# Linear attention: values by token from halves of 64 tokens, the denominator as a column of ones beside v, y transposed by DMA

## The chip, the cores and the metric

One core of one Trainium2 chip. The time is device microseconds of one execution. Before: 1068.77 us, the median of three runs (1067.99 to 1069.69).

## The reference, cut to what matters

```python
qkv = x @ W_attn + b_attn                      # x: (8, 1024, 512), after a layer norm
q, k, v = jnp.split(qkv, 3, axis=-1)           # 16 heads of 32
q = elu(to_heads(q)) + 1.0
k = elu(to_heads(k)) + 1.0
def step(carry, inp):                          # over the 1024 tokens
    kv = kv + kt[..., :, None] * vt[..., None, :]
    ksum = ksum + kt
    num = einsum('bhi,bhij->bhj', qt, kv)
    den = einsum('bhi,bhi->bh', qt, ksum)[..., None] + 1e-6
    return ((kv, ksum), num / den)
x = x + (y @ W_proj + b_proj)
x = x + ffn(layernorm(x))                      # clip, round to fp8, times fp8 weight, + bias
```

## The kernel before

The 8192 tokens are 64 tiles of 128; eight tiles are one sequence. Four tiles make a group (16 groups), for which q, k and v are computed in 12 blocks of 12 matmuls of 512 columns: the f32 operands are split into two f16 parts, and three of the four products are kept. Eight blocks give q and k with features on partitions (`phi`: ACT does exp and relu, VectorE joins them), four give v with tokens on partitions (`v_out`). The blocks of the next group are spread over the four tiles of this one, three a tile (A, B and C below; `ahead`).

A tile n does this. `scores`: per head k times q, 32 features, the result S with key tokens on partitions and 128 query tokens on columns, four PSUM banks, one per head h of a group g. The mask: VectorE takes head 0 with a product, ACT copies heads 1 to 3 and POOL masks them in place (L941). `values`: first state times q (from the second tile of a sequence on), then v times the masked scores, into Y, 128 columns of the same four banks; features on partitions. `update`: the tile's k and v give a 32 x 32 addition to each head's state, for which `k_tokens` has transposed k; in the last tile of a sequence both are left out. VectorE multiplies Y with the inverse denominators (L703) into y. ACT copies y's high part (yh), POOL makes the low one (yl), `proj` multiplies them with W_proj in 12 matmuls. VectorE adds x and takes statistics (L604 to L609), POOL norms (L909, L911) and adds a bias (L957), ACT makes fp8 and bf16 copies (`t2`), a DMA transposes, `ffn` multiplies, ACT copies, VectorE adds (L720), SyncE stores. `ln1` and `ln1_parts` do the layer norm of tile n + 8 and its two f16 parts (POOL norms, ACT copies the high part, VectorE the low one, L621), which a DMA transposes into xt, four tiles at once.

The denominator of a group before: VectorE scans k along the tokens (L647, L649), POOL multiplies the sums with q (L936), four matmuls with a matrix `pick` sum over a head's features (`den`), ACT copies, VectorE inverts (L656); the inverse is split into three bf16 parts (`den_rest`, `den_third`, `den_top`, `den_middle`), and four matmuls with `lend` spread them over partitions (`lend_out`), ACT copies them to rden.

The order of every engine is written out by hand; waits are on semaphores. On PE a tile's order is: scores(n), block A, block B, (in a group's first tile spreading), k_tokens(n + 1), block C, values(n), update(n), proj(n - 1), ffn(n - 2). scores(n + 1) waits for y(n). The PSUM has four banks R, taken in turn by every other product (`take`), and the four of S. On SyncE's queue: transposes of xt (four at a group's end), x2's transpose, the load of x for tile n + 10, the store of tile n - 2, each behind its wait. In the head the maxima of the three parts of W_attn are taken by VectorE (L732), scales are made (L741 to L751) and the weights are split; in tile 0 VectorE has W_proj's low part (L797) and four steps on the FFN weight (L803 to L816).

## Time and profile before

| | us |
|---|---|
| median of 3 runs | 1068.77 |
| profiled execution | 1068.26 |
| its span, first to last instruction | 1066.4 |
| TensorE (PE) busy | 995.8 (93%) |
| VectorE (DVE) busy | 772.3 (72%) |
| GpSimd (POOL) busy | 715.0 (67%) |
| ScalarE (ACT) busy | 570.8 (54%) |
| granted TensorE clock, mean | 0.985 |

The profile has the start and the duration of every instruction of one execution. PE is the matmuls, PEld the weight loads beside them; ends of matmuls are modelled, and they overlap, so start-to-start differences are used for their pace. A f32 matmul call leaves two records. In a timeline, each row is a start, a duration, engine, line, operation, output and inputs, and a count of merged records; brackets show how long the engine was idle before it and which instruction ended that.

### The profile page before, as it was taken

How to read it: one execution, taken by the hardware profiler on the slowest of the kernel's cores; microseconds unless marked ns; L12 is line 12 of the kernel's file. 1: busy time of each engine (PE TensorE's matmuls, PEld its weight loads, DVE VectorE, ACT ScalarE, POOL GpSimd, SP SyncE). 2: the span in 40 equal slices, each digit the busy share in tenths (PEclk: the TensorE clock that was granted, in tenths of full speed). 3: DMA queues.
4: the chain of work that ended last, by engine and by line, in shares of the span. 5: the costliest groups of instructions: out<-in, count | busy, mean ns of one | idle time of the engine just before them, and what ended most of it. 6: DMA issues, size and time to landing. Idle time of an engine off the chain costs nothing.

```text
span 1066.4 us, 27817 instructions
## 1 busy us (share of the span) xinstructions
PE 995.8 (93%) x11456; PEld 508.4 (48%) x11456; DVE 772.3 (72%) x1279; ACT 570.8 (54%) x937; POOL 715.0 (67%) x717
## 2 busy tenths in 40 slices
PE   5866999999999999999999999999999999999986
PEld 2323454455545545454544555455454554445542
DVE  7895777778777776877777687777767777775655
ACT  4444455564646555474655647465564746546442
POOL 4343969776785867678587767758667785864444
PEclk9988999999999999999999999999999999999989
DMA  8401131324123131313323231321313123121011
GB/s 263 102 1 41 46 71 41 76 52 80 46 61 70 42 75 51 80 41 66 61 51 76 51 72 44 71 60 51 76 51 67 49 65 66 41 66 31 22 41 51
DMA packets 121935, 65.78 MB, mean 62 GB/s; under 512 B 102480, under 2 KB 102480, under 8 KB 121808
## 3 DMA queue, kind: packets, MB, share of 16 engines
q1 hardware_dynamic: 121808, 63.99, 25.3%
q8 instruction: 91, 1.49, 0.6%
q14 instruction: 36, 0.29, 0.1%
HBM read 22.81 MB, written 16.78 MB: 37 GB/s over the span
## 4 chain that ended last, share of the span: by engine, by line
PE 49%; POOL 30%; DVE 11%; ACT 5%; issue 3%; DMA 1%; SPq 0%; POOLq 0%; DVEq 0%; ACTq 0%
PE R L220 40%; POOL sm L941 9%; POOL st L909 6%; PE S L220 5%; POOL xs L957 5%; POOL xs L926 4%; POOL xn L911 3%; POOL x L911 3%; DVE xs L710 3%; DVE st L604 3%; PE S L308 2%; ACT rel L445 1%; ACT qkv L442 1%; PE R L224 1%; ACT xnhl L430 1%
## 5 line engine op out<-in xcount | busy, mean ns | idle before, releaser
L220 PE MATMUL R<-xt,wh 128*128 128x512 f16 x960 | 289.2, 383 | 14.0 <-ACT rel L445 14.0
L627 DVE SCALAR_TENSOR_TENSOR qkv<-qkv,rel 128x512 f32<-128x512 f32 x128 | 117.3, 917 | 142.2 <-ACT rel L445 142.1
L941 POOL TENSOR_SCALAR_AFFINE_SELECT sm<-sm 128x512 f32<-128x512 f32 x184 | 181.5, 1014 | 5.4 <-ACT sm L430 5.4
L220 PE MATMUL R<-xt,wl 128*128 128x512 f16 x480 | 183.2, 382 | 0.0
L909 POOL TENSOR_TENSOR st<-st,half 128x1 f32<-128x1 f32 x128 | 93.5, 731 | 133.3 <-DVE st L609 127.4
L936 POOL TENSOR_TENSOR cum<-cum,qkv 128x512 f32<-128x512 f32 x64 | 88.0, 1375 | 102.0 <-DVE cum L647 56.1
L220 PE MATMUL R<-wh,xt 128*128 128x512 f16 x480 | 150.3, 379 | 0.0
L220 PEld LDWEIGHTS R<-xt,wh 128*128 128x128 f16 x960 | 89.4, 98 | 120.7 <-ACT rel L445 17.5
L442 ACT ACTIVATE qkv<-R,bqk,wm 128x512 f32<-128x512 f32 x128 | 99.5, 777 | 69.6 <-PE R L220 68.7
L948 POOL TENSOR_TENSOR yl<-y,yh 128x512 f16<-128x512 f32 x64 | 74.9, 1170 | 80.0 <-ACT yh L430 79.1
L430 ACT ACTIVATE yh<-y 128x512 f16<-128x512 f32 x64 | 40.3, 630 | 136.8 <-DVE y L703 136.8
L430 ACT ACTIVATE sm<-S 128x512 f32<-128x512 f32 x184 | 96.9, 598 | 29.4 <-PE S L308 29.1
L621 DVE TENSOR_TENSOR xnhl<-xn,xnhl 128x512 f16<-128x512 f32 x60 | 74.8, 1247 | 33.3 <-ACT xnhl L430 33.2
L926 POOL TENSOR_TENSOR xs<-xs,bp 128x512 f32<-128x512 f32 x64 | 95.5, 1492 | 4.7
L445 ACT ACTIVATE rel<-R,bqk,wm 128x512 f32<-128x512 f32 x128 | 98.5, 769 | 0.0
L710 DVE SCALAR_TENSOR_TENSOR xs<-R,wm,xs 128x512 f32<-128x512 f32 x64 | 48.0, 750 | 66.6 <-PE R L220 66.6
L604 DVE BATCH_NORM_STATS2 st<-xs 128x6 f32<-128x512 f32 x128 | 88.4, 690 | 6.5 <-DMA xs<-in_L_attn_x 4.2
L220 PE MATMUL R<-wl,xt 128*128 128x512 f16 x240 | 91.0, 379 | 0.0
L430 ACT ACTIVATE o<-R 128x512 f16<-128x512 f32 x64 | 38.2, 596 | 97.8 <-PE R L220 97.8
L220 PE MATMUL S<-sm,qkv 128*32 128x128 f32 x2048 | 77.5, 277 | 12.2 <-POOL sm L941 12.1
L308 PE MATMUL S<-qkv 32*128 32x128 f32 x2048 | 77.4, 289 | 9.4 <-DVE y L703 9.4
L957 POOL TENSOR_TENSOR xs<-xs,bf 128x512 f32<-128x512 f32 x64 | 81.7, 1276 | 5.3
(107 smaller groups left out, 1705.8 us busy)
## 6 DMA issues: line engine op xcount, KB each, us to landing
xs<-in_L_attn_x SPq DMA_DIRECT2D x64, 256.0 KB, 3.1
out<-xs SPq DMA_DIRECT2D x64, 256.0 KB, 2.0
qkv<-in_L_attn_W_attn SPq DMA_DIRECT2D x3, 1024.0 KB, 7.9
xs<-in_L_attn_W_proj SPq DMA_DIRECT2D x4, 256.0 KB
rden<-in_L_ffn_weight SPq DMA_DIRECT2D x1, 1024.0 KB, 14.7
x2t<-x2b SPq DMA_TRANSPOSE x62, 2.4
xt<-xnhl SPq DMA_TRANSPOSE x60, 3.2
bv<-in_L_attn_b_attn SPq DMA_DIRECT2D x1, 256.0 KB, 8.1
```

Source lines behind the costliest of these rows:

```text
L220: return e.matmul(out, a, b, start=start, stop=stop, skip_group_check=True)
L308: mm = e.matmul(S[:, h, g * P:(g + 1) * P], src[rows, 4 + g, cols], src[rows, g, cols], start=True, stop=True)
L430: return e.activation(out, in_, ACT.Copy, **more)
L442: e.activation(dst[:, i, :], bank["qkv", j, i][:, :], ACT.Exp, scale=UN[i // 4], bias=bqk[:, i:i + 1])
L445: e.activation(rel[:, u % 2, :], bank["qkv", j, i][:, :], ACT.Relu, scale=UN[i // 4], bias=bqk[:, i:i + 1]).then_inc(s_relu, 1)
L604: e.bn_stats(row[:, 0:6], src).then_inc(s_bn, 1)
L627: e.scalar_tensor_tensor(qkv[j % 2][:, i, :], qkv[j % 2][:, i, :], 1.0, rel[:, (u - 1) % 2, :], ALU.min, ALU.add).then_inc(s_phi, 1)
L909: e.tensor_tensor(row[:, 10:11], row[:, 9:10], half[:, :], ALU.pow).then_inc(s_rs, 1)
L926: e.tensor_tensor(x, x, bp[:, :], ALU.add).then_inc(s_xb, 1)
L936: e.tensor_tensor(c, c, qkv[j % 2][:, g, :], ALU.mult).then_inc(s_qc, 1)
L941: e.affine_select(out=four(sm[:, h, :]), in_=four(sm[:, h, :]), compare_op=ALU.is_ge, fill=0.0, base=0, pattern=[[0, 4], [1, P]], channel_ ...
L957: e.tensor_tensor(x, x, bf[:, :], ALU.add).then_inc(s_x1b, 1)
```

## The change

- Tokens lie on the partitions of the result. A tile is two halves of 64 tokens. `scores` gives for each half its own 64 x 64 block, in two column strips. A half's effect on the next one goes through the state: `update` gives an addition for each half, VectorE makes `mid` (the state after the first half) and `state`. `from_state` multiplies q of each half with the state before that half.
- v has a column of ones beside each head (`W` = 33 columns), so the state has the sums of k as a 33rd column, and Y has the denominator as a 33rd column. VectorE adds epsilon, inverts 16 numbers a partition and multiplies. The scans, `den`, the inverse's parts and `lend_out` are gone; k_tokens and update are made for all tiles.
- y has tokens on partitions and its two parts are transposed by a DMA (`t_y` on SyncE). For the last four tiles PE transposes y and ACT and VectorE make the parts.
- ACT copies two of four heads' scores in one instruction and POOL masks them with a product; VectorE masks the other two. In the last four tiles VectorE masks all.
- update moves to the tile before, `proj` stands behind `values` in the last group too. xt has two buffers, and is transposed one tile at a time, behind y's transpose on SyncE's queue.
- Head: ACT measures the size of the first two parts of W_attn and of W_proj (a sum of absolute values), VectorE keeps the maximum for v, now ahead of `scale(1)`; POOL clips the FFN weight and makes the low parts of x for tiles 4 to 7. `ffn_low` stands ahead of tile 0, `ffn_high` in it ahead of values, `ffn_round` behind update(1), `ffn_sum` in tile 1. ACT's `ffn_half` and `proj_weight` stand ahead of tile 0.

```diff
 NT = B * T // P
 NB = NT // 4
...
         UN_V, UN_P = wm[:, 33:34], wm[:, 34:35]
-        raw = qkv[1][:, :, :].rearrange("p a n -> p (a n)").rearrange("p (k n) -> p k n", k=4)
         raw_p = xs[:, NX - 4:NX, :]
-        xt0 = sm[:, :, :].rearrange("p a n -> p (a n)").bitcast(F16).rearrange("p (k n) -> p k n", k=8)
-        w_f = rden[1][:, :, :]
...
-                for h in heads:
-                    out = take(("lent", 4 * j + h), s_rden, 4 * j + h + 1)
-                    pe.wait_ge(s_lend, 4)
-                    pe.wait_ge(s_third, j + 1)
-                    matmul(out[:, :], lend[:, h, :], inverse(j)[2], True, True).then_inc(s_lent, 1)
-
...
+            def update(n):
...
+                passes = n % PER < PER - 1
+                out = [take(("delta", n, 0), s_mid, n + 1)]
+                if passes:
+                    out.append(take(("delta", n, 1), s_state, state_count(n)))
...
+                for g in range(4):
+                    for a in range(len(out)):
+                        rows = tokens(n, a)[1]
+                        for h in range(4):
+                            at = 4 * g + h
+                            mm = matmul(out[a][32 * h:32 * h + 32, g * W:(g + 1) * W],
+                                        ktok[rows, n % 2, 32 * at:32 * at + 32], v[rows, c, at, :], True, True)
+                mm.then_inc(s_delta, 1)
...
-                    for h in range(4):
-                        rows = slice(32 * h, 32 * h + 32)
-                        mm = e.matmul(S[:, h, g * P:(g + 1) * P], src[rows, 4 + g, cols], src[rows, g, cols],
-                                      start=True, stop=True)
-                        if g == 3:
-                            mm.then_inc(s_score, 1)
...
-                for g in range(4):
-                    for h in range(4):
-                        at = (4 * g + h) * 32
-                        mm = matmul(out[32 * h:32 * h + 32, 32 * g:32 * g + 32], ktok[:, n % 2, at:at + 32],
-                                    src[:, 8 + c, at:at + 32], True, True)
...
+                    for a in range(2):
+                        cols, out = tokens(n, a)
+                        for h in range(4):
+                            rows = slice(32 * h, 32 * h + 32)
+                            matmul(S[out, h, g * HALF:(g + 1) * HALF], src[rows, 4 + g, cols], src[rows, g, cols], True, True)
...
+                for a in range(1 if first else 0, 2):
+                    cols, out = tokens(n, a)
+                    held = mid if a else state[:, n % 2, :]
                     for g in range(4):
                         for h in range(4):
                             rows = slice(32 * h, 32 * h + 32)
-                            matmul(Y[32 * g:32 * g + 32, h, :], state[rows, n % 2, 32 * g:32 * g + 32],
-                                   src[rows, g, cols], True, False)
+                            mm = matmul(Y[out, h, g * W:(g + 1) * W], src[rows, g, cols], held[rows, g * W:(g + 1) * W],
+                                        g == 0, False)
+                            if a == 1 and g == 3:
+                                mm.then_inc(s_score, 1)
+
+            def values(n):
...
                 for h in range(4):
-                    if h >= dve_heads(n):
-                        pe.wait_ge(s_sel, masked_act(n, h))
                     for g in range(4):
-                        col = (4 * g + h) * 32
-                        mm = matmul(Y[32 * g:32 * g + 32, h, :], src[:, 8 + c, col:col + 32],
-                                    sm[:, h, g * P:(g + 1) * P], first, True)
+                        for a in range(2):
+                            rows = tokens(n, a)[1]
+                            mm = matmul(Y[rows, h, g * W:(g + 1) * W], sm[rows, h, g, :], v[rows, c, 4 * g + h, :],
+                                        first and a == 0 and g == 0, True)
                 mm.then_inc(s_av, 1)
+
+            def t_y(n):
+                out = take(("ty", n), s_ytl, n - NT + 5)
+                pe.wait_ge(s_y, n + 1)
+                transposes(out, [y[:, h * P:(h + 1) * P] for h in range(4)]).then_inc(s_ty, 1)
 
...
-                    mm = matmul(out[:, :], yl[:, n % 2, g * P:(g + 1) * P], wph[:, g, :], False, g == 3)
...
+                    pe.wait_ge(s_yt[n % 2], 16 * (n // 2 + 1))
+                mms = [(a + h, b, h) for a, b in ((0, wph), (0, wpl), (4, wph)) for h in range(4)]
+                for i, (k, b, h) in enumerate(mms):
+                    mm = matmul(out[:, :], yt[:, n % 2, k, :], b[:, h, :], i == 0, i == 11)
...
                 proj_qkv(0, i)
-                if i in (0, 2):
-                    most(1 if i == 0 else 2)
-            k_tokens(0)
-            den(0)
-            most(3)
+                if i in (0, 2, 8):
+                    most((0, 2, 8).index(i) + 1)
+                if i == 9:
+                    k_tokens(0)
+            update(0)
             for n in range(NT + 2):
...
                 if n < NT:
                     scores(n)
+                    from_state(n)
                     ahead(j + 1, 3 * c)
-                    if j + 1 == NB:
-                        proj(n - 1)
...
-                    if c == 0:
-                        lend_out(j, (0, 1))
...
+                if n <= NT and tail(n - 1):
+                    t_y(n - 1)
...
-                    if c == 0:
-                        lend_out(j, (2, 3))
                     values(n)
-                    update(n)
-                if 1 <= n < NT and j + 1 < NB:
+                    if n + 1 < NT:
+                        update(n + 1)
+                if 1 <= n <= NT:
                     proj(n - 1)
                 if n >= 2:
+                    t2(n - 2)
                     ffn(n - 2)
...
             def scores(n):
-                for h in range(dve_heads(n), 4):
-                    act.wait_ge(s_score, 4 * n + h + 1)
+                if not tail(n):
+                    act.wait_ge(s_score, 4 * n + 4)
                     if n:
                         act.wait_ge(s_av, n)
-                    else:
-                        act.wait_ge(s_qkv, 12)
-                    copy(sm[:, h, :], S[:, h, :]).then_inc(s_scopy, 1)
+                    copy(sm[:, 2:4, :, :], scored(2)).then_inc(s_scopy, 1)
...
             def scores(n):
-                for h in range(dve_heads(n)):
...
+                for i, h in enumerate((0, 2) if tail(n) else (0,)):
...
-                    e.tensor_tensor(four(sm[:, h, :]), four(S[:, h, :]), over(causal[:, :]),
-                                    ALU.mult).then_inc(s_smd, 1)
+                    e.tensor_tensor(sm[:, h:h + 2, :, :], scored(h), causal_over(2), ALU.mult).then_inc(s_smd, 1)
 
...
+                    e.tensor_copy(mid[:, :], fresh).then_inc(s_mid, 1)
+                else:
                     dve.wait_ge(s_state, state_count(n - 1))
-                new, old, fresh = state[:, (n + 1) % 2, :], state[:, n % 2, :], bank["delta", n][:, 0:P]
-                if n % PER == 0:
-                    e.tensor_copy(new, fresh).then_inc(s_state, 1)
-                else:
-                    e.tensor_tensor(new, fresh, old, ALU.add).then_inc(s_state, 1)
+                    e.tensor_tensor(mid[:, :], fresh, old, ALU.add).then_inc(s_mid, 1)
+                if n % PER < PER - 1:
+                    dve.wait_ge(s_mid, n + 1)
+                    e.tensor_tensor(new, bank["delta", n, 1][:, 0:4 * W], mid[:, :], ALU.add).then_inc(s_state, 1)
...
+                e.tensor_scalar(inv, out[:, :, :, 32:33], DEN_EPS, None, ALU.add).then_inc(s_den, 1)
+                dve.wait_ge(s_den, n + 1)
+                e.reciprocal(den[:, :], den[:, :]).then_inc(s_dinv, 1)
...
-                e.tensor_tensor(four(y[:, :]), Y, rden[j % 2][:, :, c * P:(c + 1) * P],
-                                ALU.mult).then_inc(s_y, 1)
+                e.tensor_tensor(y[:, :].rearrange("p (h g i) -> p h g i", h=4, g=4), out[:, :, :, 0:32],
+                                inv.broadcast_to([P, 4, 4, 32]), ALU.mult).then_inc(s_y, 1)
+
...
-            for g in range(4):
-                denominators(0, g)
-                v_out(0, g)
-            parts_less()
-            proj_peak()
-            invert(0)
-            den_rest(0)
+            ffn_low()
+            v_out(0, 0)
+            v_out(0, 1)
             proj_scale()
-            den_third(0)
+            v_out(0, 2)
+            v_out(0, 3)
+            update(0)
...
-                    if j + 1 == NB:
-                        proj(n - 1)
+                    if n == 1:
+                        ffn_sum()
...
-                    if n == 0:
-                        ffn_low()
...
-                    if c == 3 and j + 1 < NB:
-                        invert(j + 1)
...
-                    update(n)
-                    if c == 3 and j + 1 < NB:
-                        den_rest(j + 1)
-                if 1 <= n < NT and j + 1 < NB:
+                    if n + 1 < NT:
+                        update(n + 1)
+                    if n == 0:
+                        ffn_round()
+                if 1 <= n <= NT:
                     proj(n - 1)
                 if n >= 2:
...
-                for h in range(dve_heads(n), 4):
-                    pool.wait_ge(s_scopy, masked_act(n, h))
-                    e.affine_select(out=four(sm[:, h, :]), in_=four(sm[:, h, :]), compare_op=ALU.is_ge, fill=0.0,
-                                    base=0, pattern=[[0, 4], [1, P]], channel_multiplier=-1).then_inc(s_sel, 1)
+                if not tail(n):
+                    pool.wait_ge(s_scopy, n + 1)
+                    e.tensor_tensor(sm[:, 2:4, :, :], sm[:, 2:4, :, :], causal_over(2), ALU.mult).then_inc(s_sel, 1)
...
+            for k in range(4):
+                e.tensor_scalar(w_f[:, k, :], w_f[:, k, :], 448.0, -448.0, ALU.min, ALU.max).then_inc(s_wfc, 1)
...
+                    if n + 8 < NT:
                         add_bp(n + 8)
-                    scores(n)
...
-                    after(j + 1, 3 * c + 2)
                     values(n)
...
+            def t_y(n):
...
+                    sp.wait_ge(s_yl, n + 1)
+                    if n >= 2:
+                        sp.wait_ge(s_proj, n - 1)
+                    e.dma_start(yt[:, n % 2, :, :], yhl[:, n % 2, :, :].rearrange("p a n -> p (a n)"),
+                                transpose=True).then_inc(s_yt[n % 2], 16)
...
             for n in range(NT + 2):
-                j, c = divmod(n, 4)
-                last = c == 3 and j + 2 < NB
-                if last:
-                    t1(4 * j + 8)
-                    t1(4 * j + 9)
+                if 1 <= n <= NT:
+                    t_y(n - 1)
...
+                if n + 8 < NT:
+                    t1(n + 8)
                 if n >= 2:
                     t2(n - 2)
...
-                if n == 0:
-                    sp.wait_ge(s_wfd, 5)
```

## Rows read from the trace of the kernel before

**Rows 1.** The page: the span, and busy time, share and instructions of two engines
```profile
span 1066.4 us, 27817 instructions
...
PE 995.8 (93%) x11456; PEld 508.4 (48%) x11456; DVE 772.3 (72%) x1279; ACT 570.8 (54%) x937; POOL 715.0 (67%) x717
```
**Rows 2.** Windows: three tiles; busy us and instructions per engine, clock, DMA
```profile
577.05:593.04 15.99, 15.32 (x157) 7.95 (x156) 10.91 (x19) 11.87 (x20) 10.26 (x11) 1.00 0.18 54
...
623.71:639.56 15.85, 15.85 (x193) 7.95 (x192) 11.98 (x19) 6.36 (x11) 9.43 (x11) 1.00 0.53 94
982.97:997.68 14.71, 14.71 (x185) 7.88 (x184) 9.65 (x14) 7.33 (x12) 8.86 (x9) 1.00 0.10 29
```
**Rows 3.** Waits from 184 to 960 us: total us, times, longest
```profile
PE S L220 <- POOL sm L941: 10.3, 23, 0.6
...
PE R L220 <- ACT rel L445: 8.1, 12, 0.7
```
**Rows 4.** Timelines of the head, PE first, then DVE: start us, us, instruction
```profile
31.00 0.55 PE L220 MATMUL R<-ident,wm 128*128 128x128 f32 x2 [4.37 <-DVE wm L732]
...
59.01 1.06 PE L220 MATMUL R<-cum,pick 128*32 128x512 f32 x8 [2.12 <-POOL cum L936]
61.22 0.46 PE L220 MATMUL R<-ident,wm 128*128 128x128 f32 x2 [1.15 <-DVE wm L732]
61.61 1.17 PE L308 MATMUL S<-qkv 32*128 32x128 f32 x32
...
90.68 2.09 PE L308 MATMUL S<-qkv 32*128 32x128 f32 x32 [9.40 <-DVE y L703]
...
28.57 2.28 DVE L732 TENSOR_REDUCE wm<-qkv 128x1 f32<-128x2048 f32 x1
...
76.67 3.35 DVE L797 SCALAR_TENSOR_TENSOR wpl<-xs,wm,wph 128x2048 f16<-128x2048 f32 x1
...
83.83 2.61 DVE L811 SCALAR_TENSOR_TENSOR x<-x 128x2048 fp8e4<-128x2048 fp8e4 x1 [0.89 <-ACT x L430]
```
**Rows 5.** Timeline of PE at the tail: scores of tile 60
```profile
1013.54 1.17 PE L308 MATMUL S<-qkv 32*128 32x128 f32 x32
```
**Rows 6.** Timelines of PE in windows 992.39:992.49, 982.97:983.86, 993.72:993.94 (records started)
```profile
992.39 0.39 PE L220 MATMUL S<-qkv,state 32*32 32x128 f32 x16
...
982.97 1.15 PE L308 MATMUL S<-qkv 32*128 32x128 f32 x29
...
993.72 0.43 PE L220 MATMUL R<-qkv,ktok 128*32 128x32 f32 x28
```
**Rows 7.** Groups of weight loads by line: busy us, mean ns, idle before
```profile
L308 PEld LDWEIGHTS S<-qkv 32*128 32x128 f32 x2048 | 64.9, 191 | 36.3 <-issue 26.3 <-DVE y L703 9.9
...
L220 PEld LDWEIGHTS R<-qkv,ktok 128*32 128x32 f32 x1792 | 26.5, 111 | 0.0
```
**Rows 8.** Timeline of PE in a late tile
```profile
992.39 0.50 PE L220 MATMUL S<-qkv,state 32*32 32x128 f32 x32
992.82 1.10 PE L220 MATMUL S<-sm,qkv 128*32 128x128 f32 x32
993.72 0.48 PE L220 MATMUL R<-qkv,ktok 128*32 128x32 f32 x32
994.13 1.04 PE L220 MATMUL R<-wph,yh 128*128 128x512 f16 x4
```
**Rows 9.** Timeline of POOL in a tile of the steady state
```profile
594.31 0.93 POOL L909 TENSOR_TENSOR st<-st,half 128x1 f32<-128x1 f32 x1 [0.61 <-DVE st L609]
...
598.93 1.59 POOL L926 TENSOR_TENSOR xs<-xs,bp 128x512 f32<-128x512 f32 x1
600.48 3.64 POOL L941 TENSOR_SCALAR_AFFINE_SELECT sm<-sm 128x512 f32<-128x512 f32 x3
```
**Rows 10.** DMA issues by kind: KB each, median us from issue to landing
```profile
x2t<-x2b SPq DMA_TRANSPOSE x62, 2.4
```

More of the change, by code:

```diff
@@ L19 @@
 P = 128
+HALF = P // 2
+W = 33
 NT = B * T // P
@@ L158, in build @@
         s_xt = [sem(f"xt{t}") for t in range(4)]
+        s_yt = [sem(f"yt{i}") for i in range(2)]
         s_x2t = [sem(f"x2t{i}") for i in range(2)]
-        s_t1, s_qkv, s_den, s_lent, s_score = sem("t1"), sem("qkv"), sem("den"), sem("lent"), sem("score")
-        s_ktr, s_delta, s_av, s_proj = sem("ktr"), sem("delta"), sem("av"), sem("proj")
-        s_ffn, s_t2, s_most = sem("ffn"), sem("t2"), sem("most")
-        s_xth, s_wh, s_relu, s_whi = sem("xth"), sem("wh"), sem("relu"), sem("whi")
@@ L525, in values @@
             def values(n):
-                act.wait_ge(s_y, n + 1)
-                if n >= 2:
-                    act.wait_ge(s_proj, n - 1)
-                copy(yh[:, n % 2, :], y[:, :]).then_inc(s_yh, 1)
+                if not tail(n):
+                    act.wait_ge(s_y, n + 1)
+                    if n >= 2:
+                        act.wait_ge(s_yt[n % 2], 16 * (n // 2))
+                    copy(yhl[:, n % 2, 0, :], y[:, :]).then_inc(s_yh, 1)
+            def t_y(n):
+                act.wait_ge(s_ty, n - NT + 5)
+                act.wait_ge(s_proj, n - 1)
+                copy(yt[:, n % 2, 0:4, :], four(bank["ty", n][:, :])).then_inc(s_yth, 1)
             def ffn(n):
@@ L537, in ahead, with t1 @@
             def ahead(j, s):
-                if j < NB:
-                    if s < 8:
-                        phi(j, ORDER[s])
-                    if s == 10:
-                        den(j)
-            for m in range(4):
-                act.wait_ge(s_t1, m + 1)
-                copy(xt0[:, 0:4, m * P:(m + 1) * P], four(bank["t1", m][:, :])).then_inc(s_xth, 1)
+                if j < NB and s < 8:
+                    phi(j, ORDER[s])
+            def t1(m):
+                act.wait_ge(s_t1, m + 1)
+                copy(xt[0][:, 0:4, m * P:(m + 1) * P], four(bank["t1", m][:, :])).then_inc(s_xth, 1)
+            t1(0)
+            t1(1)
+            t1(2)
+            attn_size(0)
+            t1(3)
             attn_weight(0)
             attn_weight(1)
+            attn_size(1)
             phi(0, 0)
@@ L967, in _ @@
             e.memset(half[:, :], -0.5).then_inc(s_half, 1)
+            for i in range(2):
+                e.memset(v1[i][:, :, :, 32:33], 1.0).then_inc(s_one, 1)
             for m in range(4):
```

456 lines of the change are left out of this document (174 added, 282 removed).

## The prediction

> **What bounds the kernel now.** I read the page first [rows 1]: TensorE (PE) is busy for 93% of the span, VectorE (DVE) for 72%, the others for less. Ends of matmuls are modelled, so the 93% alone proves little. The pace of the tiles says more. [rows 2] cut one group of four tiles where the scores of a tile begin: 15.99 us for its first tile, 15.85 for its last, and 639.56 - 577.05 = 62.51 for the four. The last row there is a tile late in the run, where GpSimd (POOL) has no more layer norms of later tiles to make: 14.71 us, with PE busy in all of it. So 14.71 us is what PE needs for a tile. [rows 3] name the waits that make up the rest: between 184 and 960 us PE stood idle 10.3 us behind POOL's masking of scores and 8.1 us behind ACT's relu. In a group, 4 x 14.71 = 58.85 are tiles, 15.85 - 14.71 = 1.14 the sums of the denominator, four spreading matmuls of 512 columns (512 / 2.4 = 213 ns and 3 between) another 0.87: 60.9. The other 1.6 are waits. PE is the bound, and all waits together are under 3%.
>
> The head is another matter: tile 0's scores begin at 61.61 us and tile 1's at 90.68 [rows 4], 29.07 us for one tile. The tail, from tile 60's scores to the end, is 1066.4 - 1013.54 = 52.9 us [rows 1, 5].
>
> **The change part by part.** The sum stands against the profiled execution's own 1068.26 us, of which 1066.4 are span and 1.9 lie around it; the median of the runs is 0.5 higher.
>
> *How small f32 matmuls run.* One call is two records. [rows 6] show stages cut short: of the state products (32 x 32 of the array) 16 records start within 0.10 us, 6.6 ns apart. Of the scores (four row strips; 128 columns moving, 128 of weights) 29 start in 0.89 us: eight rounds of four, 0.111 each. Of the state's update (four column strips; 32 columns of each) 28 start in 0.22 us: eight rounds of 0.032. So a round costs the longer of moving (two cycles of 2.4 GHz a column: 107 ns for 128, 27 ns for 32) and weights, plus 4 to 5 ns, and each array tile runs by itself. [rows 7]: a weight load takes 191 ns for 128 columns of f32 and 111 for 32, about 0.83 ns a column, so 64 columns have 53 ns. Behind a stage whose shape is left lie 0.11 to 0.2 us more.
>
> *Scores and state products.* Each is 32 calls now, 64 records, 64 columns of weights, 64 or 33 moving, on 4 x 2 array tiles. A round of eight is 0.057, each stage 0.46, one change of shape behind both: 1.05 us. Before they took 1.11 (the 0.89 of [rows 6] and 0.22 behind it) and 0.43 [rows 8]. **-0.49 us a tile.** The bound from above is the dearest row of a short record, the update with what lies behind it, 0.41 / 32 = 12.8 ns: 128 x 12.8 = 1.64, +0.10.
>
> *Values.* 32 calls with 64 rows and 64 columns of weights, 33 moving. Only the two array tiles of the diagonal are used, so it is 32 rounds of 0.057 = 1.83, plus 0.12 behind, as the update has another shape now: 1.95 against 0.90 [rows 8]. **+1.05.** Bounds: if weights didn't count, the update's round, 32 x 0.032 + 0.12 = 1.14 (+0.24); if the two tiles ran in turn, 64 x 0.057 + 0.12 = 3.77 (+2.87). I take 0.057, since in the scores' round weights and moving are equally long and neither adds to the other.
>
> *Update.* 32 calls on eight array tiles, 64 records at 6.6 ns and what lies behind: 0.57 against 0.41 [rows 8]. **+0.16.** Together +0.72: **14.71 + 0.72 = 15.43 us a tile.** In every eighth tile half the state product and in another half the update is missing, 14 x 0.22 = -3 us over the run.
>
> *Denominator and spreading, gone.* On PE 1.14 + 0.87 us a group; 15.43 is already without them. The scans, reciprocals, products and copies of DVE, POOL and ACT lie beside PE and bring nothing but the waits of [rows 3]. DVE gets two small operations and one more state addition a tile (some 0.2 us each); POOL masks by one product instead of 3.64 us of three selects [rows 9].
>
> *What is late next.* Count from the start of a tile's scores. PE: scores and state 1.05, blocks A and B 6.2, key transposes 6.7, C 9.3, values 11.25, update 11.8, proj 14.4, ffn 15.4. POOL's mask waits in its queue behind ln2 of the last tile, whose statistics DVE has at 1.3, and behind ln1: some 4.3 us (from 594.31 to the addition at 598.93, less a wait between, [rows 9]), and the product takes 1.6 like that addition: done at 7.2, needed at 9.3. DVE: phi C to 12.2, denominators and y to 13.4, states to 14.0; needed at 15.4. SyncE's queue now has y's transpose, then xt's, which waits for DVE's low parts (7.4), then x2's. y's own starts behind the store of the last tile but two (which waits for DVE's addition, about 2 us into the next tile) and lands at 6.7, needed at 11.8. x2's is issued when ACT has its copy, at 9.9, 1.2 us of issue and 2.4 to landing [rows 10]: 13.5, needed at 14.5. So every margin is 1 us or more. Where one goes, the tile costs what a wait costs now, 0.6 us (15.34 against 14.71). I take 0.1 a tile, 6 us; bounds 0 and 0.6.
>
> *Head.* PE waits 4.37 us up to 31.00 for the third weight's scale, because DVE takes its maximum (28.57) behind two phis; matmuls start at half pace behind that stall for some 3.5 us (clock 1.2 instead of 2.4 GHz). The maximum now comes ahead of the second scale: -4.4 and -1.5. A wait of 2.12 us for POOL's sums, den's 1 us and another wait for a scale lie between 59.01 - 2.12 and 61.61 [rows 4]; they go, while phi(7), the FFN weight's first part and v on one DVE queue hold block 10 for 1.1, and the update of tile 0 waits for the last block. Scores(0) then begin at 52.9: **-8.7.** In tile 0 DVE's queue sets y(0): 3.35 us for proj's weight, 2.61 and more for the FFN weight [rows 4]. Afterwards: phi A 6.1, low parts 7.4, phi B 8.9, proj's weight 12.3, phi C 13.0, the 2.6 to 15.6, y and states to 16.8. **16.8 - 29.07 = -12.3**, with PE still idle for 4.3 of it. Tile 1: no ffn (-0.95), half clock at its start (+1.5).
>
> *Tail.* Tiles 60 to 62 have no blocks; PE's own work is 8.3 us each and the chain of proj, statistics, ln2, two copies and a transpose sets about 9.5; with the masks on DVE alone and y transposed by PE the last tile has one more copy in its chain and less masking. I leave the tail at its 52.9 us [rows 1, 5]. **0, give or take 4.**
>
> *Sum.* Tile 1 begins at 52.9 + 16.8 = 69.7. 59 tiles of 15.43 are 910.4; +0.5 (tile 1), -3, +6 (waits): tile 60 at 983.6. With 52.9 and 1.9: **1038 us.**
>
> **The rivals.** (a) *Issue is the bound; slower.* No stage of now has more than 32 records at 6.6 ns in a row; scores and state products have 128. If a record costs 12.8 ns in a long row, then scores, state and update are 192 x 12.8 = 2.46, with values 4.41 against 2.85 now, 16.27 a tile: +50, **1088**. The sign turns where these four stages pass 4.1 us. Against it speak the 28 records in 0.22 us right behind 64 others [rows 6]; for it, that no row shows a longer stretch. The Trainium skill, page "TensorE: Matmul & The Clock Gate", section "Wait — 56ns, not 53.3ns?", says that starts are never closer than about 25 ns, however few the columns. The rows here show 13 ns for a call of two records. By the page, an estimate: 96 calls x 25 ns = 2.4 us, the same 1088.
>
> (b) *The two tiles of the diagonal exclude each other; slower.* Both row strips write bank h together, while now each row strip has its own bank. Values take 3.77: 1.83 x 59 = +108, **1146**. Against: writes last 27 ns of a round that weights hold to 57, so that writes in turn would still fit. The Trainium skill has a rule for it, page "TensorEngine Tiling", section "Gotcha 1: PSUM Pressure": different row tiles cannot access the same PSUM bank at the same time. No row here shows such a case.
>
> (c) *Weights of 64 columns don't count.* Values 1.14: -0.81 x 59, **990**. Against: [rows 7].
>
> (d) *A new wait in most tiles,* x2's transpose behind xt's, or y behind phi C: 0.6 for 0.1, +30 and something for the tail: **1073**. For it: margins of 1 us are thin.
>
> (e) *The steady pace isn't moved* (15.63 as now) and only the head is gained: 1068.3 - 21 = 1047, within the forecast's range.
>
> **How the numbers follow.** Forecast with (e) 0.60, its own range 1018 to 1062; (a) 0.16, (b) 0.08, (c) 0.07, (d) 0.09. The range leaves (b) and (c) out and takes (a) with its spread: 1012 to 1100. A measurement of this kernel tells 0.2% (2 us) from no change. Faster: 0.57 of the forecast's and (c), 0.64; same 0.04; slower 0.32.
>
> **What would show it.** Tile 0's scores at 53 us, tile 1's at 70. In a late tile, start to start: scores and state 1.05, values 1.95, update 0.57, the tile 15.4 to 15.6, no idle PE behind POOL's mask. (a) would show as scores and state over 1.6, (b) as values of 3.8, (d) as PE idle by over 0.5 us ahead of ffn or scores in most tiles. A pace over 15.9 us would make the sign wrong.

## The result and the profile after

The changed kernel took 1076.62 us, the median of 4 runs (1074.19 to 1077.97), the kernel before 1069.19 on the same chip: ratio 1.0069, 95% interval 1.0048 to 1.0089. Slower by 0.7%, where the forecast was 1038. The profiled execution had 1077.97, of which 1076.2 are span.

The page of the changed kernel, its first lines, with queue 8, which brings instructions, and the chain that ended last:

```profile
span 1076.2 us, 43457 instructions
...
PE 1048.8 (97%) x19504; PEld 616.9 (57%) x19504; DVE 648.9 (60%) x1319; ACT 458.3 (43%) x715; POOL 534.8 (50%) x524
...
q8 instruction: 153, 2.51, 1.0%
...
PE 93%; DVE 2%; POOL 1%; ACT 1%; issue 1%; DMA 1%; POOLq 0%
```

VectorE, ScalarE and POOL have less to do than in [rows 1], as the change says; PE has more: 19504 records for 11456, and 53 us of busy time more. The waits of [rows 3] are gone; between 184 and 960 us PE waits for nobody. But the pace did not fall. Windows of three whole tiles (columns as in [rows 2]):

```profile
584.16:600.33 16.17, 16.17 (x314) 9.57 (x313) 10.19 (x20) 8.30 (x13) 8.29 (x8) 1.00 0.30 72
...
972.52:988.69 16.17, 16.17 (x313) 9.57 (x312) 6.67 (x15) 7.71 (x12) 5.34 (x5) 1.00 0.16 43
988.69:1004.86 16.17, 16.17 (x313) 9.57 (x313) 6.81 (x15) 6.35 (x10) 5.33 (x5) 1.00 0.17 44
```

16.17 us with PE busy throughout, mid-run and late, for 14.71 unhindered and some 15.6 with waits before [rows 2]. Timelines of PE show the head, the tail and one tile:

```profile
54.92 0.81 PE L212 MATMUL S<-qk 32*64 32x64 f32 x53
70.18 0.41 PE L212 MATMUL S<-qk 32*64 32x64 f32 x8 [2.89 <-DVE y L649]
1021.03 0.31 PE L212 MATMUL S<-qk 32*64 32x64 f32 x8
```
```profile
966.29 2.06 PE L212 MATMUL S<-v,sm 64*64 64x33 f32 x64
968.27 0.76 PE L212 MATMUL R<-v,ktok 64*32 64x33 f32 x64
968.97 1.04 PE L212 MATMUL R<-wph,yt 128*128 128x512 f16 x4
...
972.52 0.86 PE L212 MATMUL S<-qk 32*64 32x64 f32 x60
973.16 0.21 PE L212 MATMUL S<-state,qk 32*64 32x33 f32 x1
...
974.15 0.39 PE L212 MATMUL R<-xt,wh 128*128 128x512 f16 x1
```

Start to start: values 968.27 - 966.29 = 1.98, update 0.70, scores and state 974.15 - 972.52 = 1.63. The same stages cut short, in windows 972.52:972.75 and 968.27:968.47, have the records that started by then:

```profile
972.52 0.44 PE L212 MATMUL S<-qk 32*64 32x64 f32 x25
...
968.27 0.35 PE L212 MATMUL R<-v,ktok 64*32 64x33 f32 x32
```

25 records of the scores in 0.23 us are 9 ns each, 32 of the update in 0.20 us 6 ns each.

The whole difference of the two profiled executions is then: head 70.18 - 90.68 = -20.5 [rows 4]; 59 tiles 1021.03 - 70.18 = 950.9 for 922.9 before [rows 4, 5], +28.0; tail 55.2 for 52.9, +2.3. Together +9.8, against 1076.2 - 1066.4 = 9.8 between the spans.

### The profile page after: what moved, and what is told of

Its sections match the earlier page's. It is cut to its first block, busy times and chain, and to the rows that moved or that the text cites. A ratio compares the mean times of both kernels' runs of the same rounds, so it can differ in the third digit from the quotient of the medians.

```text
span 1076.2 us, 43457 instructions
## 1 busy us (share of the span) xinstructions
PE 1048.8 (97%) x19504; PEld 616.9 (57%) x19504; DVE 648.9 (60%) x1319; ACT 458.3 (43%) x715; POOL 534.8 (50%) x524
## 4 chain that ended last, share of the span: by engine, by line
PE 93%; DVE 2%; POOL 1%; ACT 1%; issue 1%; DMA 1%; POOLq 0%
PE R L212 70%; PE S L212 21%; PE R L216 3%; POOL st L838 1%; DVE st L578 0%; POOL xn L840 0%; DMA x2t<-x2b 0%; DVE xs L661 0%; DVE sm L618 0%; POOL xnhl L853 0%; DMA xs<-in_L_attn_x 0%; DVE wl L716 0%; DVE raw L755 0%; ACT qk L426 0%; ACT wh L417 0%
## 5 line engine op out<-in xcount | busy, mean ns | idle before, releaser
L212 PE MATMUL R<-xt,wh 128*128 128x512 f16 x1024 | 307.1, 382 | 2.4 <-ACT wh L417 2.4
L601 DVE SCALAR_TENSOR_TENSOR qk<-qk,rel 128x512 f32<-128x512 f32 x128 | 131.1, 1025 | 170.1 <-ACT rel L429 170.0
L872 POOL TENSOR_TENSOR yhl<-y,yhl 128x512 f16<-128x512 f32 x60 | 70.1, 1168 | 322.0 <-ACT yhl L417 322.0
L426 ACT ACTIVATE qk<-R,bqk,wm 128x512 f32<-128x512 f32 x128 | 99.5, 777 | 121.4 <-PE R L212 121.3
L212 PEld LDWEIGHTS S<-v,sm 64*64 64x64 f32 x4096 | 124.5, 135 | 28.6 <-issue 25.4
L212 PE MATMUL R<-wph,yt 128*128 128x512 f16 x512 | 132.9, 382 | 2.0 <-DVE yt L654 2.0
L212 PE MATMUL S<-v,sm 64*64 64x33 f32 x4096 | 131.6, 221 | 2.3 <-DVE sm L618 2.3
L417 ACT ACTIVATE yhl<-y 128x512 f16<-128x512 f32 x60 | 37.8, 631 | 165.5 <-DVE y L649 165.5
L595 DVE TENSOR_TENSOR xnhl<-xn,xnhl 128x512 f16<-128x512 f32 x56 | 86.3, 1540 | 19.5 <-ACT xnhl L417 19.5
L212 PEld LDWEIGHTS R<-xt,wl 128*128 128x128 f16 x512 | 50.4, 98 | 61.4 <-issue 1.7
L212 PEld LDWEIGHTS R<-wh,xt 128*128 128x128 f16 x512 | 50.3, 98 | 56.4 <-issue 1.6
```

Source lines behind the costliest of these rows:

```text
L212: return e.matmul(out, a, b, start=start, stop=stop, skip_group_check=True)
L417: return e.activation(out, in_, ACT.Copy, **more)
L426: e.activation(dst[:, i, :], bank["qkv", j, i][:, :], ACT.Exp, scale=UN[i // 4], bias=bqk[:, i:i + 1])
L595: e.tensor_tensor(xnhl[:, m % 4, 1, :], xn[:, m % 2, :], xnhl[:, m % 4, 0, :], ALU.subtract).then_inc(s_xlo, 1)
L601: e.scalar_tensor_tensor(qk[j % 2][:, i, :], qk[j % 2][:, i, :], 1.0, rel[:, (u - 1) % 2, :], ALU.min, ALU.add).then_inc(s_phi, 1)
L872: e.tensor_tensor(yhl[:, n % 2, 1, :], y[:, :], yhl[:, n % 2, 0, :], ALU.subtract).then_inc(s_yl, 1)
```

## Experiments

All times beside "before" are from the same chip as the run they stand with. e2, e4, e7 and e8 are single runs. A "train" is a row of short products with nothing wide between them; a "stage" is one of a tile's steps on PE (scores and state, values, update, projection).

**e1 and e2: is it the order of the loops or the number of records?** In the state products the halves are the outer loop, so that only four array tiles follow each other, not the eight that the forecast counted. e1 puts them inside:

```diff
-for a in range(1 if first else 0, 2):
-    ...
-    for g in range(4):
-        for h in range(4): ...
+for g in range(4):
+    for a in range(1 if first else 0, 2):
+        ...
+        for h in range(4): ...
```

> The state products loop over g outside and the halves inside, so that eight array tiles follow each other instead of four; nothing else. Theory of tiles and queue: a record costs the round (57 ns for 64 columns of weights) over the number of array tiles that follow each other, and behind the first 32 records of a run not under 8.3 ns. The changed kernel's state products used four tiles (14.3 ns a record). Now 32 x 7.2 + 96 x 8.3 + 130 ns = 1.16 us for scores and state together against 1.63, in 56 of 64 tiles: -26 us, 1050. Rival, issue alone at 12 to 13 ns a record: nothing moves, 1077.

Measured 1067.78 (10 runs), before 1067.80: ratio 1.0003, 0.9991 to 1.0015. In the trace:

```profile
709.73 0.85 PE L212 MATMUL S<-qk 32*64 32x64 f32 x60
...
711.20 0.39 PE L212 MATMUL R<-xt,wh 128*128 128x512 f16 x1
```

1.47 for the 128 records. The order is worth 0.16 us a tile and 7 to 9 us in all (7 by the ratios to before, 9 by the medians, which are from different chips); 1.47 is still 0.42 over the forecast's 1.05, with eight array tiles in turn. It lies between the two values expected, 1.16 and 1.63, and bears neither theory out. e2 does the reverse in `scores`:

```diff
-for g in range(4):
-    ...
-    for a in range(2): ...
+for a in range(2):
+    for g in range(4): ...
```

> The scores loop over the halves outside, so that only four array tiles follow each other; nothing else. Tiles and queue: 64 records at 57 / 4 = 14.3 ns, 0.91 us against 0.70 up to the state's first record, +0.22 x 64 = +14 us, 1091. Issue alone: no change, 1077.

1082.66 in one run; the stage takes 1.73 for 1.63. The expectations were 0.22 us more and none; measured is 0.10. So four array tiles in turn cost 0.1 to 0.16 us a stage. The other 0.42 us is not the loops' order; it goes with the stage of 128 records, as rival (a) had it, but neither run shows why.

**e8: does a shorter train run faster?** The update's 64 records in two trains of 32, the second behind the projection.

```diff
-update(n + 1)
+update(n + 1, (0, 1))
 ...
 proj(n - 1)
+update(n + 1, (2, 3))
```

> The changed kernel with the update's 64 records issued as 32 ahead of the projection and 32 behind it. Theory of the queue (about 32 records start at 7 ns each, and only what follows them is paced by issue): each half's starts lie within 0.23 us, and the two halves take about 0.25 to 0.39 each with their last product, against 0.69 in one; the time is 1074 to 1080. Rival (the array's tiles pace the update, 9 to 11 ns a record whatever is queued): each half's starts spread over 0.29 to 0.35 us.

1087.34 in one run. Timeline of PE:

```profile
715.98 0.36 PE L212 MATMUL R<-v,ktok 64*32 64x33 f32 x32
...
718.96 0.36 PE L212 MATMUL R<-v,ktok 64*32 64x33 f32 x32
```

The next stage begins 0.29 us behind each start: 0.58 for what takes 0.69 in one. That is the update of the forecast (0.57). As expected, 32 records start within 0.2 us; in the one train of the changed kernel the first 32 start within 0.16 us and the last at 0.57 (medians of its tiles). The time, expected at 1074 to 1080, rose, by 9.4 us between the profiled executions. The projection now has 2.69 us from its start to the next stage's, not 2.60, so that most tiles take 16.16 for 16.17; PE waits six times, 4.7 us in all, for "issue" in `scores` and state; the tail is 2.4 us longer (57.6 for 55.2); and the tile of each sequence in which the update has only 32 records takes 16.1 for 15.87. The waits for issue belong to the next question but one.

**e4: do the two array tiles of the diagonal exclude each other?** The values' products, all of the first half, then all of the second, so that only one array tile is at work.

```diff
-for h in range(4):
-    for g in range(4):
-        for a in range(2): ...
+for a in range(2):
+    for h in range(4):
+        for g in range(4): ...
```

> Values does all calls of the first half, then all of the second: one array tile at a time, same calls. If the two diagonal tiles run beside each other in the changed kernel though they write the same bank: 64 x 57 ns + 0.12 = 3.77 us against 1.98, +1.79 x 64 = +115 us, 1192. If they take turns already (the rule on banks): no change, 1077.

1229.43 in one run:

```profile
706.61 3.71 PE L212 MATMUL S<-v,sm 64*64 64x33 f32 x64
710.25 0.83 PE L212 MATMUL R<-v,ktok 64*32 64x33 f32 x64
711.01 1.89 PE L212 MATMUL R<-wph,yt 128*128 128x512 f16 x4
...
726.04 3.71 PE L212 MATMUL S<-v,sm 64*64 64x33 f32 x64
729.68 0.76 PE L212 MATMUL R<-v,ktok 64*32 64x33 f32 x64
730.37 1.04 PE L212 MATMUL R<-wph,yt 128*128 128x512 f16 x4
```

3.64 in turn, 1.98 side by side, though both write the same bank. Rival (b) is out. The Trainium skill, page "TensorEngine Tiling", section "Gotcha 1: PSUM Pressure", forbids row tiles to share a bank at one time; in this kernel the two overlap and lose no time by it. The run is 37 us over the expectation, and 24 tiles of 59 account for that: they take some 19.5 us for 17.8. Behind the long narrow stage, in which PE used one array tile, the granted clock falls there to the lower level, 1.2 GHz. Windows (PE busy, clock, DMA): the first begins with the slow projection above, the second with the fast one.

```profile
711.01:714.20 3.19, 3.19 (x13) 0.51 0.03 5
730.37:732.97 2.60, 2.60 (x19) 1.00 0.02 6
```

**e3: do the weights' columns set the values?** Each values product in two of 32 columns, 128 records instead of 64, on four array tiles; the loops are those of the changed kernel:

```diff
-mm = matmul(Y[rows, h, g * W:(g + 1) * W], sm[rows, h, g, :], v[rows, c, 4 * g + h, :], ...)
+for b in range(2):
+    at = a * HALF + b * 32
+    mm = matmul(Y[at:at + 32, h, g * W:(g + 1) * W], sm[rows, h, g, b * 32:b * 32 + 32], v[rows, c, 4 * g + h, :], ...)
```

> Each call of values is split into two with 32 columns of weights, on two column strips: 64 calls, four array tiles, the shape of the update behind it. Tiles and queue: a round of four is 33 ns (weights 27), 8.2 ns a record, about the queue's 8.3, so 128 records take 1.07 us, no drain behind, the update 0.66: 1.73 against 2.67, -0.94 x 63 = -59 us, 1018. Issue alone at 12.6 ns: 1.61 + 0.8, -17 us, 1060. If weights are loaded one column strip after the other, nothing is won: 1077 or more.

1119.91 (4 runs), ratio 1.0489 (1.0466 to 1.0513). Timelines of two tiles, then the waits of the whole run (us in total, times, longest):

```profile
705.85 1.41 PE L212 MATMUL S<-v,sm 64*32 64x33 f32 x128
707.11 0.75 PE L212 MATMUL R<-v,ktok 64*32 64x33 f32 x64
...
720.97 1.40 PE L212 MATMUL S<-v,sm 64*32 64x33 f32 x128
722.22 0.55 PE L212 MATMUL R<-v,ktok 64*32 64x33 f32 x40
724.96 0.33 PE L212 MATMUL R<-v,ktok 64*32 64x33 f32 x24 [2.19 <-issue]
```
```profile
PE R L212 <- issue: 49.1, 28, 2.6
...
PE S L212 <- issue: 5.8, 8, 1.3
```

The narrower weights work: values in 1.26 for 1.98, and a whole tile without a wait takes 15.47 for 16.17 (the first of a sequence, which lacks half of the state products, 15.25 for 15.85). The records of such a train start at an even pace, the first 32 in 0.26 us and all 128 in 1.10 (medians of e10, which has the same train), 8.6 ns each; so a train of 128 need not take the 11.5 ns a record of scores and state in e1. The time expected was 1018, or 1060 if issue alone set the pace; it is 1120, because in other tiles PE stops in the middle of a train. No semaphore is waited for; the row says "issue".

**Where the waits stand.** I numbered TensorE's instructions (records, weight loads, waits of their own) in the order in which they started. In e3, e6, e8, e9, e10, e11 and e14 there are 84 waits for "issue" of over 0.5 us between 100 and 1060 us, and every one stands ahead of a number that leaves 193 on division by 256; I call these places borders. Each ended 1.1 to 1.6 us after one of queue 8's packets of 16384 bytes had landed. In e3, for one, a border lies in the values at 721.31; a packet starts at 722.11 and lands at 723.50, and PE goes on from the next border at 724.96. Windows between three waits of e3, from the first record behind one to the next wait, show it without numbering:

```profile
724.96:742.92 17.96, 15.78 (x382) 9.11 (x383) 10.07 (x20) 8.29 (x14) 8.05 (x9) 1.00 0.35 69
742.93:762.53 19.60, 17.48 (x383) 9.43 (x382) 10.45 (x20) 6.94 (x11) 8.81 (x9) 0.91 0.30 61
```

765 records and loads in either, and three waits of PE's own: 768 = 3 x 256. The Trainium skill, page "Runtime: NRT & Kernel Launch", section "Instruction fetch mechanics", says that instructions come in blocks of 16 KiB, 256 of them; the trace agrees. It also says that the fetch is hidden because issue is slower than the fetch; here it isn't. A train of 128 records has 256 instructions with its weight loads and passes in 1.26 us. Borders at which PE waited lie 2.3 to 7.9 us behind the last one, the middle one 3.6, wait included; without the wait itself 81 of the 84 lie under 3.5 us behind it. In the kernel before no two borders between 100 and 1000 us are nearer than 5.7 us by the same count. Nearness alone isn't the whole rule: the changed kernel has 13 borders under 3.5 us behind the last, the nearest 1.8, and waits at none.

**e6, e9, e10, e11: spread the trains.** All have e1's loop order. e6 is e3's values with the projection between values and update; e9 has only two of the four banks in 32 columns; e10 and e11 also have the projection there and move the tile's third block of wide products (C) behind the update, on ACT and VectorE too, e10 with all four banks, e11 with two. The order of a tile's end in e6 and in e10, e11:

```diff
 # e6
 values(n)
-update(n + 1)
 proj(n - 1)
+update(n + 1)
 ...
 # e10, e11
-ahead(j + 1, 3 * c + 2)
 values(n)
-update(n + 1)
 proj(n - 1)
+update(n + 1)
+ahead(j + 1, 3 * c + 2)
```

> The changed kernel with the halves inside the loop over heads' groups in the products with the state (as in e1), the values' products in two of 32 columns (as in e3), and the output projection moved between the values' products and the next tile's update, so that 128 records of values and 64 of update are no longer one train. Theory (the waits for issue in e3 come from trains of some 200 and more short instructions that outrun the instruction fetch): they go, a tile takes about 15.1, and the time is 1018 to 1030. Rival (the fetch falls behind over whole stretches, in step with the transposes by DMA, whatever the order inside a tile): waits for issue of some 50 us in all stay, 1080 to 1110.

> e1 with the values' products of two of the four banks in two of 32 columns, 96 records in place of 64. Theory of tiles and issue: values take the mean of 1.98 and 1.26, 1.62, a tile 0.36 less than in e1, and the time is 1067.8 - 64 x 0.36 = 1045. If the waits for issue grow with the instructions of a tile as a whole (e3 had 37 for 64 records more): half of e3's 52 us, about 1070. If they have a threshold that lies above this number, none.

> e6 with each tile's third group of 12 wide products (2.6 us) moved from ahead of the values to behind the update, on TensorE, ScalarE and VectorE. Every train of short products (scores and state 128 records, values 128, update 64) then has at least 2.6 us of wide products on both sides. Theory (an uninterrupted stretch of more than about 192 records with their weight loads outruns the fetch, and 1 us of wide products between is too little to catch up): the waits for issue (24 us in e6) all but go in the tiles 1 to 60, a tile takes 8.31 + 1.35 + 1.47 + 0.69 + 2.60 + 0.96 = 15.4, and the time is 1030 to 1040. Rival (the fetch is short over a tile as a whole): some 20 us of such waits stay, 1055 to 1075. A third case: the values stand 2.6 us earlier and wait for the masked scores, up to 2.6 us a tile, over 1100.

> The same order with the values' products of two banks in 32 columns and of two in 64 (96 records, as e9, whose values took 1.74). By the theory no wait for issue, a tile of 8.31 + 1.74 + 1.47 + 0.69 + 2.60 + 0.96 = 15.8, and 1055 to 1060; by the rival 1065 or more.

| | median us (runs) | ratio to before | "issue" waits of the profiled run |
|---|---|---|---|
| e6 | 1073.32 (7) | 1.0057 (1.0034 to 1.0079) | 24.9 us |
| e9 | 1071.82 (10) | 1.0046 (1.0024 to 1.0067) | 9.3 us |
| e10 | 1064.46 (10) | 0.9964 (0.9941 to 0.9988) | 24.4 us |
| e11 | 1064.50 (10) | 0.9963 (0.9948 to 0.9978) | 1.1 us |

The times of one kernel vary by up to 11 us from one execution to the next (e9 1066.7 to 1077.6, the profiled one the fastest). e6's waits fell by half, and 25 of 31 now stand in scores and state; the projection between the trains isn't enough, and the time lies between its theory (1018 to 1030) and the rival (1080 to 1110). e9 has the time of the case in which waits grow with the instructions (about 1070), but 9.3 us of them in the profiled run, for 26 expected. e11 all but loses the waits, as its theory said, with tiles of 15.88 and 4.5 us more than its 1055 to 1060. e10 has tiles of 15.36 and tiles of 17 to 19.5; it came out where its rival had it, with some 20 us of waits and 1055 to 1075, and 24 us over the theory's 1030 to 1040. So distance between trains alone doesn't free a kernel of the waits. Two of its tiles:

```profile
417.87 1.28 PE L212 MATMUL S<-v,sm 64*32 64x33 f32 x128
421.46 1.04 PE L212 MATMUL R<-wph,yt 128*128 128x512 f16 x4 [2.31 <-issue]
...
435.29 1.42 PE L212 MATMUL S<-v,sm 64*32 64x33 f32 x128
436.64 0.60 PE L212 MATMUL R<-wph,yt 128*128 128x512 f16 x2
```

The same stages, with and without the wait. By the numbering the values of the first begin exactly on a border, those of the second 181 instructions behind one.

**e12, e13, e14: move the borders.** If that is the cause, the place of the borders can be set by counting. e12 and e13 have e10's order, one or two values products kept at 64 columns so that eight tiles have a multiple of 256 instructions, and 59 or 18 small products ahead of everything:

```diff
+for _ in range(59):          # 18 in e13
+    matmul(R[0][0:32, 0:32], ident[0:32, 0:32], ident[0:32, 0:32], True, True)
 for m in range(4):
     t1(m)
```

> What the traces so far show: numbering TensorE's instructions in the order in which they started (matmul records, weight loads, waits of their own), all 79 waits for issue inside trains of short products, in six kernels, stand ahead of a number that leaves 193 on division by 256. In e10 a tile has some 756 such instructions, so that the place of these borders moves by 12 a tile and by 76 in two tiles of eight, and the tiles that wait are those in which the values begin 0 to 50 (or 244 to 255) instructions behind a border; no tile with 83 to 220 waits over 0.3 us. This kernel is e10 with one or two of the 32 values' products of a tile kept at 64 columns, so that eight tiles have 5888 = 23 x 256 instructions, and with 59 small products by the identity ahead of everything, in time in which TensorE waits for its first input. By this the values begin at 215, 199, 183, 167, 151, 135, 55 and 231 behind a border in each sequence of eight. Theory (instructions come in blocks of 256, and a border that follows too soon on the last waits): nearly no waits for issue in tiles 1 to 60, a tile 15.4 in the mean, and the time 1028 to 1040. Rival (the number 193 is a coincidence of counting, waits come by the number of short products alone): as e10, 1064, some 24 us of waits.

> The same kernel with 18 in place of the 59 small products ahead of everything, 164 instructions fewer, nothing else. The values then begin at 51, 35, 19, 3, 243, 227, 147 and 67 behind a border in each sequence of eight. Theory of the blocks: three to five tiles of eight wait some 2 us each, 24 to 40 waits, 50 to 80 us in all, 1080 to 1110, with the same instructions in the tiles as e12. Rival: no difference from e12 beyond the head's 0.7 us.

e12 1064.97 (12 runs, ratio 0.9973, 0.9959 to 0.9987), e13 1090.90 (4 runs, 1.0213, 1.0195 to 1.0232): 26 us between kernels whose tiles have the same instructions, and e13 has fewer of them. PE waits for "issue", first e12's main row (two more add 1.1 us), then e13's two:

```profile
PE S L212 <- issue: 8.0, 9, 1.2
```
```profile
PE S L212 <- issue: 27.2, 18, 2.0
...
PE R L212 <- issue: 2.2, 6, 1.4
```

The direction is as expected and e13's time in its range, the waits are half of what was expected (29.4 us of 50 to 80); e12's 1065 for 1028 to 1040 is the time that its rival had, but with 9.1 us of waits and not 24. In these two traces the numbers of the waits drift by some 8 from one sequence to the next. The traces show why: `ffn` has 194 matmul records for 256 weight loads in each, so about one record a tile is missing. With each matmul counted by its weight load, of which none is missing, the 26 waits for "issue" of over 0.5 us (10 and 16) stand at the same place as the 84, one of them one place on, and each ended 1.2 to 1.6 us behind a packet of queue 8. By that count the values begin some 10 places nearer to the border than planned: in e12 the first tile of a sequence, 46 to 40 behind it, waits 0.7 to 1.1 us in six of seven, in e13 mostly two tiles do, 40 to 5 behind it, 1.0 to 2.0 us each. e12's own time missed because the products kept at 64 columns cost 0.34 us each: its values take 1.56 with one and 1.91 with two, for 1.22 in e10. So e14 keeps all of them at 32 columns, has 17 of the small products ahead of everything, and makes up the count behind the update:

```diff
+for i in range(5 if n % PER == 1 else 7):
+    h = i % 4
+    mm = matmul(out[0][32 * h:32 * h + 32, 8 * W:9 * W], ktok[0:HALF, n % 2, 32 * h:32 * h + 32], v[0:HALF, c, h, :], True, True)
```

> e10 (128 records of values, all in 32 columns) with 7 small products behind each update (5 in one tile of eight), into columns that nobody reads, and 17 by the identity ahead of everything. Eight tiles then have 6151 - 8 = 6143 instructions by the numbering of e10, 24 x 256 less 1, and the values begin at 118, 134, 152, 168, 186, 139, 93 and 101 behind a border, all in the range (83 to 220) in which no tile of e10 waited. Theory of the borders: waits for issue in the tiles 2 to 60 fall from 24 us to under 3, a tile takes 15.36 + 0.12 (seven calls at 16.7 ns) = 15.5, and the time is 1036 to 1046. Rival (what matters is how many instructions there are): more of them, so 1064 + 7 = 1071 or more.

1049.94 (5 runs, 1049.18 to 1050.92), before 1067.39: ratio 0.983, 0.9817 to 0.9844. It has 898 records more than e10 in its trace, for products that nobody reads, and is 14.5 us faster.

```profile
PE R L212 <- DMA x2t<-x2b: 5.2, 13, 0.6
PE S L212 <- issue: 4.4, 8, 1.1
...
PE R L212 <- issue: 2.1, 2, 1.5
```

6.5 us of these waits for 24.4, and in the tiles 2 to 59 only 1.5, where under 3 was expected; no two borders nearer than 3.5 us between 100 and 1000 us (1.2 in e3, 1.6 in e10). It missed its 1036 to 1046 by 4 us: tiles 2 to 59 take 15.69 in the mean, 15.47 for a late one without a wait, and the transposes of x2 now come late 13 times.

**e7: the head.** v's maximum back behind two relu operations on VectorE.

```diff
-v_peak()
 scale(1)
 ...
 phi(0, 1)
+v_peak()
```

> The changed kernel with the maximum over v's columns of weights back behind the first two relu operations on VectorE, where the kernel before has it. The head's term of the prediction: the scores of tile 0 start 4 to 6 us later than 54.9, at 59 to 61, and the whole takes 1081 to 1083. Rival (ScalarE's and TensorE's own work sets the head by now): the scores stay within 1 of 54.9, and the whole at 1077.

1081.99 in one run, tile 0's scores at 58.96, 4.0 us later:

```profile
31.03 0.77 PE L212 MATMUL R<-ident,wm 128*128 128x128 f32 x2 [4.68 <-DVE wm L681]
```

The wait that the kernel before has there [rows 4] is back.

## Why the prediction was wrong

- **Head**: right in the main. Scores of tile 0 at 54.92 (forecast 52.9), of tile 1 at 70.18 (69.7), PE idle for 2.9 of it (4.3); -20.5 us for -21. That the total fits so well is in part luck: its two terms are off by +2.0 and -1.5. e7 shows one of its parts by itself.
- **Values**: right, 1.98 for 1.95. Weights of 64 columns do count (with 32 the same rounds take 1.26, e3), and the two array tiles work side by side (e4). Rivals (b) and (c) are out.
- **Waits**: 6 us were set aside, none came. Rival (d) is out.
- **Tail**: 55.2 for 52.9, within its 4.
- **Scores and state**, 1.05 forecast, 1.63 measured: the step that failed. Two readings in it were wrong. The first is small: eight array tiles in turn were taken for the state products, where the loop has four; e1 gives that 0.16. The second is the rest, 0.42: that a round's price from stages of 32 records holds for 128 in a row. The forecast had a round of eight in 0.057, 7.2 ns a record, and its 6.6 ns is from the first 16 of the state products in [rows 6]. With the better order the 128 take 11.5 each (e1: 1.47 / 128): the first 32 start within 0.27 us, 64 within 0.66, the last at 1.32, and 0.15 lies behind it (medians of e1's tiles). Already the first 32 are dearer than forecast, and what follows them is dearer still.
- **Update**: 0.70 for 0.57, the same mistake, and here the length is shown to be the reason. Its 64 records are one train; in two of 32 they take 0.29 each (e8). Its first 32 do start within the forecast's 6.6 ns each.
- **The sum**: the three stages take 0.74 us a tile more than forecast, some 43 over 59 tiles; the waits set aside give 6 back. That is the distance from 913.9 to 950.9. Rival (a) had the size, 16.27 us a tile for 16.17 measured; its 12.8 ns a record was 12.1 for scores, state and update. Its mechanism, issue as the bound, is not shown: the values of e3 and e10 issue 128 records at 8.6 ns each. What the text held against it, 28 records in 0.22 us behind 64 others, was no evidence: in the changed kernel, too, the update starts 32 records in 0.2 us right behind the values, and the stage as a whole is slower all the same.

The Trainium skill, page "TensorE: Matmul & The Clock Gate", gives TensorE a queue of 64 instructions (section "Architectural detail: the array is 16× 32×32, not 1× 128×128"). 32 records with their weight loads are 64, and the update fits a train that starts from a full queue: 32 records in 0.2 us, then slower. The other trains don't show it: of e10's values the first 32 start no faster than the rest (0.26 us, and 8.6 ns a record in all). So the queue as the reason is argued for the update alone; no run here changed the queue. The same page's floor of 25 ns between starts, cited ahead of the result, doesn't hold here: the update's first 32 records come at 13 ns a call, and with the stage's end included the values of e10 take 19 a call, the scores and state of e1 23.

What stays open: why scores and state take 11.5 ns a record where e10's values take less, since no run split that train or changed the shape of its products; the exact rule by which a border waits; and part of e14's tiles, 15.69 in the mean for 15.47, 13 us in 58 tiles, of which waits make up 8.

## What to carry to other kernels

The time of one small product has to be read from a train as long as the one that is planned, and of its shape: the cut stages of the kernel before gave 6.6 to 8 ns a record on 32-column tiles, the train of 128 took 11.5 to 12.7, and one of another shape 9.5. Where a kernel issues hundreds of short products in a row, count TensorE's instructions as well as its time: as a rule of thumb from these runs, borders every 256 of them should lie 4 us or more apart (81 of 84 waits came where they lay nearer), and spreading trains between wide products, or even a few idle products, can buy that. Here the same work came at 1076.6, 1064.5 and 1049.9 us with nothing but the order, the columns and the count of the small products changed.

## What the runs showed of the hardware

- PE waits for its own instructions: 84 of 84 waits for "issue" of over 0.5 us at a border of 256 instructions, each 1.1 to 1.6 us after a packet of instructions had landed, and 26 more in e12 and e13 by the count of weight loads. Between a border and the next lay 3.6 us in the middle case.
- f32 records on small array tiles: 32 of the update start in 0.2 us, 64 take 0.69; 128 of scores and state take 1.47, 128 of the values in 32 columns 1.22.
- Two array tiles on the diagonal write one bank at the same time: 1.98 us, and 3.64 in turn.
- Behind a stage of 3.6 us with one array tile at work the clock was granted at 0.51 (1.2 GHz) for some 3 us, in 24 tiles of 59.
- One product with 64 columns of weights among 32-column ones cost 0.34 us, two 0.69.
